# Rounds of four steps instead of two in a fused group-norm and displaced-convolution kernel

## What is computed

```python
# _gn(x): g = x in 32 groups; (g - mean(g)) / sqrt(var(g) + 1e-5)
disp = displace(_gn(x), round(offset))          # one offset for each of 48 groups of 8 channels
kernel = exp(-|field + offset - round(offset)|^2 / (2 * 0.5 ** 2)), normalised over 5 x 5
out = x + conv(disp, kernel)                    # depthwise, padding 2
```

## Time and profile before

| | us |
|---|---|
| median of 3 runs | 1166.61 |
| lowest and highest run | 1166.39, 1168.48 |
| the profiled execution | 1167.79 |
| its span in the trace | 1166.0 |

### The profile page before, as it was taken

One profiled execution on the slowest core, in us unless ns is written; L12 is line 12 of the kernel. 1 busy time (PEld: TensorE's weight loads), 2 busy tenths in 40 slices (PEclk: granted clock), 3 DMA queues, 4 the chain that ended last, 5 costly groups with the idle time before them and its releaser, 6 DMA issues.

```text
span 1166.0 us, 114171 instructions
## 1 busy us (share of the span) xinstructions
PE 1151.8 (99%) x50576; PEld 1125.5 (97%) x50576; DVE 953.2 (82%) x1373; ACT 785.5 (67%) x873; POOL 970.4 (83%) x1743
## 2 busy tenths in 40 slices
PE   9999999999999999999999999999999999999997
PEld 9899999999999999999999999999999999999997
DVE  8788888888888888888888888888888888888863
ACT  4676766667666676676767666676676766667664
POOL 7788888888888888888888888888888888888884
PEclk9999999999999999999999999999999999999999
DMA  8699999999999999999999999999999999999966
GB/s 273 237 383 382 364 355 369 359 358 358 349 360 356 355 361 352 359 355 357 355 354 358 353 357 358 352 359 356 353 356 353 358 350 363 359 347 362 353 212 211
DMA packets 409760, 402.93 MB, mean 346 GB/s; under 512 B 16528, under 2 KB 409744, under 8 KB 409744
## 3 DMA queue, kind: packets, MB, share of 16 engines
q1 hardware_dynamic: 204944, 201.41, 52.1%
q10 hardware_dynamic: 204800, 201.36, 50.0%
HBM read 201.38 MB, written 201.33 MB: 345 GB/s over the span
## 4 chain that ended last, share of the span: by engine, by line
PE 98%; issue 1%; POOL 0%; DVE 0%; DVEq 0%; POOLq 0%
PE ps L700 62%; PE ps L711 33%; PE ps L692 2%; PE ps L761 1%; DVE xin L513 0%; POOL var L308 0%; POOL rstd L310 0%; POOL ay L264 0%; POOL norm L326 0%; POOL ax L273 0%; DVE both L495 0%; POOL summands L286 0%; POOL spread L306 0%; POOL bias L312 0%; POOL inner L303 0%
## 5 line engine op out<-in xcount | busy, mean ns | idle before, releaser
L700 PE MATMUL ps<-ay,norm 32*128 32x128 f32 x24608 | 757.4, 275 | 1.0 <-DVEq L573 1.0
L700 PEld LDWEIGHTS ps<-ay,norm 32*128 32x128 f32 x24608 | 719.0, 187 | 9.7 <-ACTq L679 1.1
L485 DVE BATCH_NORM_STATS2 stats<-xin 128x6 f32<-128x512 f32 x768 | 488.7, 693 | 1.5 <-DMA xin<-in_x_dram 1.3
L624 ACT ACTIVATE y<-ps 128x1536 f32<-128x1536 f32 (+1 forms) x256 | 329.2, 1286 | 149.9 <-PE ps L700 149.7
L711 PE MATMUL ps<-ax,y 64*64 64x64 f32 x24576 | 392.1, 219 | 5.5 <-issue 5.4
L711 PEld LDWEIGHTS ps<-ax,y 64*64 64x64 f32 x24576 | 373.0, 135 | 22.6 <-issue 7.3
L326 POOL TENSOR_SCALAR norm<-xin,rstd,bias 128x768 f32<-128x768 f32 x256 | 296.5, 1159 | 104.3 <-PE ps L700 85.8
L513 DVE TENSOR_TENSOR xin<-ps,xin 128x1024 f32<-128x1024 f32 x256 | 313.2, 1224 | 82.9 <-PE ps L711 82.0
L613 ACT ACTIVATE norm<-xin,bias,rstd 128x768 f32<-128x768 f32 x256 | 263.0, 1027 | 168.6 <-DVE xin L513 82.5
L317 POOL TENSOR_TENSOR xin<-x,xin 128x512 f32<-128x512 f32 x256 | 321.0, 1276 | 7.6 <-ACT x L641 7.5
L641 ACT ACTIVATE x<-ps 128x512 f32<-128x512 f32 x256 | 150.5, 588 | 45.1 <-PE ps L711 45.0
(11 more groups left out here) (62 smaller groups left out, 273.4 us busy)
## 6 DMA issues: line engine op xcount, KB each, us to landing
xin<-in_x_dram SPq DMA_DIRECT2D x512, 384.0 KB, 6.9
out_dram<-xin ACTq DMA_DIRECT2D x512, 384.0 KB, 6.7
off<-in_L_conv_offset_dram SPq DMA_DIRECT2D x1, 48.0 KB, 3.2
```

Of the source, the lines that this page charges most:

```text
L485: nc.vector.bn_stats(stats[:, s // PAIR % RING, s % PAIR, n, :], xin[:, s].rearrange("p (g q) f -> p q f g", g=GROUPS)[:, n]).then_inc(bn_ ...
L624: nc.scalar.activation(y[:, v].rearrange("p k r a m -> p a (k r) m")[:, 0:lanes], ps[:, v, 0:lanes, 0:POS * P].rearrange("p a (n m) -> p a ...
L700: last = nc.tensor.matmul(ps[:, v, a, P * k:P * (k + 1)], norm[rows, v, r, P * k:P * (k + 1)], ay[rows, k, r, :], start=(r == 0), stop=(r ...
```

## The change

Rounds of four steps replace pairs of two. PE's outer loop (L825 after) does four first stages, in an inner loop of two passes, and then four second stages. `y` and `x2` get four homes instead of two; `ps` and `norm` keep two. Statistics, summands, sums and coefficients go by four steps: the small tiles are twice as wide. The product that sums the statistics has 72 columns instead of 36, and since it stands in the inner loop, it is done twice a round, of which DVE reads the second; its last matmul now also tells that the even first stage is done. The stores of a round stand in the next round, one before the first copy of y and one behind each of the other three. The normalisations of the next round's first two steps stand among the copies of the thirds. The column matrices (`ax`) are made in the new superblock's first round instead of at the end of the old. The tile for PE's idle products is made by ACT, and these products are fewer and narrower. Twelve loads instead of ten go out before the wait for the first products, and the extra first product behind the last step is gone.

```diff
-LEAD = 2
-AHEAD = PAIR * (LEAD + 2)
-RING = 4
-FIRST = 10
-BEHIND = 2
+QUAD = 4
+ROUNDS = STEPS // QUAD
+AHEAD = QUAD + 1
+FIRST = 12
...
+        y = sb("y", [P, QUAD, POS, R, LANES, 32])
+        x2 = sb("x2", [P, QUAD, QP, ROW])
+
+        stats = sb("stats", [P, 2, QUAD, CHUNKS, 3 * GROUPS])
+        summands = sb("summands", [P, QUAD, CHUNKS, 3 * GROUPS])
...
+        SPARE = 2
         IOTAS = 3 * LANES
...
+                    pool.wait_ge(bn_done, QUAD * CHUNKS * (quad + 1))
+
+                    if first:
+                        pool.wait_ge(stat_summed, 2)
+                    else:
+                        pool.wait_ge(y_done, QUAD * (quad - 1) + 1)
+                    number = quad + 2
...
-            def step(c, s, head, tail):
-                t, p = STEPS * c + s, STEPS // PAIR * c + s // PAIR
-                if not (tail and s + PAIR >= STEPS):
-                    normalise(t + PAIR, (s + PAIR) % STEPS, STEPS // PAIR * c + (s + PAIR) // PAIR)
-                if s % PAIR == 1:
-
-                    if not (tail and s // PAIR + LEAD + 1 >= STEPS // PAIR):
-                        make_summands(p + LEAD + 1, (s // PAIR + LEAD + 1) % RING)
-                    else:
-
-                        pool.engine_nop().then_inc(summands_ready, PAIR)
-                if s == STEPS - 1 and not tail:
-                    fill_rows(c + 1)
-                if s % PAIR == 1:
-                    if not (tail and s // PAIR + LEAD >= STEPS // PAIR):
-                        coefficients(p + LEAD, (s // PAIR + LEAD) % 2)
-                    add_third(t - 1, s - 1)
-                    add_third(t, s)
-                if s == STEPS - 1 and not tail:
-                    column_matrices(c + 1)
-            run(step)
+            coefficients(0, 0, early=1)
+
+            def one_round(c, g, first, last):
+                t, s, quad = STEPS * c + QUAD * g, QUAD * g, ROUNDS * c + g
+                if not first:
+                    add_third(t - 2, (s - 2) % STEPS)
+                normalise(t + 2, s + 2, quad, first)
+                if not first:
+                    add_third(t - 1, (s - 1) % STEPS)
+                if g == 0 and not first:
+                    column_matrices(c)
+                normalise(t + 3, s + 3, quad, first)
+                if last:
+
+                    pool.engine_nop().then_inc(summands_ready, QUAD)
+                else:
+                    make_summands(quad + 1, (g + 1) % 2, first=first)
+                    if first:
+                        pool.sem_inc(summands_ready, 2)
+                    coefficients(quad + 1, (g + 1) % 2, used=not first)
+                    normalise(t + 4, (s + 4) % STEPS, quad + 1)
+                    if g == ROUNDS - 1:
+                        fill_rows(c + 1)
+                    normalise(t + 5, (s + 5) % STEPS, quad + 1)
+                add_third(t, s)
+                add_third(t + 1, s + 1)
+                if last:
+                    add_third(t + 2, s + 2)
+                    add_third(t + 3, s + 3)
+            run(one_round)
...
+            def one_round(c, g, first, last):
+                t, s, quad = STEPS * c + QUAD * g, QUAD * g, ROUNDS * c + g
+                group_follows = c is not NSUPER - 1
+                for f in range(s + AHEAD, s + AHEAD + QUAD):
+                    if f >= STEPS and not group_follows:
+                        continue
+                    if f % QUAD == 0:
+
+                        if first:
+                            dve.wait_ge(first_summands, 2)
+                        else:
+                            dve.wait_ge(summands_ready, QUAD * quad + 2)
+                    all_statistics(c + f // STEPS, f % STEPS)
+                if group_follows:
+                    if g == 0:
+                        whole_distances(c + 1)
+                    if g == 1:
+                        full_distances(c + 1)
+                    if g == 3:
+                        values(c + 1)
+                if last:
+                    nc.vector.engine_nop().then_inc(sums_ready, QUAD)
+                else:
+                    sums(quad + 1, (g + 1) % 2, t + 2, read=not first)
+                copy_last_lane(t + 3)
+                if g == ROUNDS - 1 and group_follows:
+                    fill_image(c + 1)
+                for j in range(QUAD):
+                    add_x(t + j, s + j)
...
+                store_of_last_round(0)
+                copy_y(t, 0, first)
+                normalise(t + 2, s + 2, quad, first)
+                copy_y(t + 1, 1, first)
+                store_of_last_round(1)
+                normalise(t + 3, s + 3, quad, first)
+                copy_y(t + 2, 2, first)
+                store_of_last_round(2)
+                copy_y(t + 3, 3, first)
+                store_of_last_round(3)
+                border = g == ROUNDS - 1 and group_follows
                 if border:
                     fill_rows(c + 1, 0)
-                if s % PAIR == 1:
-                    copy_third(t - 1, s - 1, head and s == 1)
+                copy_third(t, s, first)
+                if not last:
+                    normalise(t + 4, (s + 4) % STEPS, quad + 1)
+                copy_third(t + 1, s + 1, first)
                 if border:
                     fill_rows(c + 1, 1)
-                    copy_third(t, s)
-                    normalise(t + PAIR, (s + PAIR) % STEPS, STEPS // PAIR * c + (s + PAIR) // PAIR, False)
-                if s >= BEHIND:
-                    store(c, s - BEHIND, t - BEHIND)
-                elif not head:
-                    store(c - 1, s - BEHIND + STEPS, t - BEHIND)
-                if not border and not (tail and s + PAIR >= STEPS):
-                    normalise(t + PAIR, (s + PAIR) % STEPS, STEPS // PAIR * c + (s + PAIR) // PAIR, False)
-                if s % PAIR == 1 and not border:
-                    copy_third(t, s, head and s == 1)
-                if not tail:
-                    if s == 5:
-                        square(c + 1, 0)
-                    if s == 7:
-                        square(c + 1, 1)
-                    if s == 9:
-                        exponential(c + 1)
-            run(step)
-
-            act.wait_ge(norm0_ready, TOTAL)
-            act.sem_inc(norm0_ready, 1)
-            act.wait_ge(mats_ready[0], TOTAL)
-            act.sem_inc(mats_ready[0], 1)
-            for s in range(STEPS - BEHIND, STEPS):
-                store(NSUPER - 1, s, TOTAL - STEPS + s)
+                copy_third(t + 2, s + 2, first)
+                if last:
+                    store(c, s, t)
+                else:
+                    normalise(t + 5, (s + 5) % STEPS, quad + 1)
+                copy_third(t + 3, s + 3, first)
+                if last:
+                    for j in range(1, QUAD):
+                        store(c, s + j, t + j)
+            run(one_round)
...
+                    last = nc.tensor.matmul(ps[:, v, a, place], ones[rows, :],
+                                            summands[rows, part].rearrange("p t n s -> p (t n s)"),
+                                            start=True, stop=True)
+                if early is None:
+
+                    last.then_inc(y_done, 1)
+                else:
+                    last.then_inc(stat_summed, 1)
...
+            def first_stages(one, number):
+
+
+                after = pe.snap(number + 1)
                 pe.wait_ge(x2_ready, one)
                 pe.wait_ge(result1_ready, one)
-                pe.wait_ge(norm0_ready, two)
-                y_product(0, 1)
-                pe.wait_ge(norm1_ready, two)
-                y_product(1, 1)
-                y_product(2, 1)
+                pe.wait_ge(y_ready, number)
+                y_even(number)
+                pe.wait_ge(summands_ready, number)
+                sum_stats(0)
+                second = pe.snap(one + 1)
+                pe.wait_ge(x2_ready, second)
+                pe.wait_ge(result1_ready, second)
+                pe.wait_ge(y_ready, after)
+                y_odd(after)
+
+            def second_stages(one):
                 pe.wait_ge(ax_ready, one)
                 pe.wait_ge(sums_ready, one)
-                pe.wait_ge(y_ready, one)
+                pe.wait_ge(y_ready, pe.snap(one + 4))
                 pe.sem_inc(x_started, 1)
                 x_products(0)
                 pe.wait_ge(last_lane_ready, one)
...
+                two = pe.snap(one + 2)
                 pe.wait_ge(x2_ready, two)
                 pe.wait_ge(result1_ready, two)
-                begin_even(three)
+                pe.sem_inc(x_started, 1)
+                x_products(2)
+                three = pe.snap(one + 3)
+                pe.wait_ge(x2_ready, three)
+                pe.wait_ge(result1_ready, three)
+                pe.sem_inc(x_started, 1)
+                x_products(3)
...
-                            nc.tensor.matmul(ps[:, v, a, POS * P + 36:512], idle[rows, :], idle[rows, 0:92],
```

(18 more changed lines are left out.)

309 lines of the change are left out of this document (144 added, 165 removed).

## The result

The changed kernel takes **1219.8 us** (median of 4 runs, 1218.6 to 1221.1) beside 1167.5 for the kernel before on the same chip: ratio 1.0448, 95% interval 1.0435 to 1.0461. That is 52 us slower, where I had forecast 6 us faster. The page of the profiled execution (span 1218.6): busy times, instruction packets, chain by engine, and the groups of the first stage's matmuls and weight loads.

A forecast was written before the change was run, and what follows sets the result against it. PE, busy 99% of the span, was taken as the bound. The terms -25.0 + 3.8 + 13.6 + 6.9 - 3.6 - 1.3 gave -5.6, so 1162.2, less 1.2: 1161 us, range 1154 to 1168.

The forecast's parts named there:

- (a): PE's stream: half of the shape changes between stages go, saving 0.39 us a round; -25.0 us (-18 to -32).
- (b): PE's sum product gets 72 columns, as often as before: 0.03 us a product, +3.8 us (0 to +7.7).
- (c): Within first stages, PE waits 0.22 us before y of t+3 for ACT's norm: +13.6 us (0 to +20).
- (d): Coefficients late for the second stages: PE waits 0.11 us before the round's last one, power taken as 1.84 us; +6.9 us.
- (e): Superblock borders: the late pair goes (-6.6), ACT's matrix fills delay copies of thirds (+3.0); -3.6 us.
- (f): Start: two instruction fetches in PE's first second-stage pass, and a wait behind a held load gone; -1.3 us (-5 to +4).
- (g): Hidden work: slot reuse after stores, DMA traffic at 357 GB/s, and DVE and POOL work stay covered, at no cost.
- the first: Rival: coefficients come in time (power near 1.02 us or a shorter chain), (d) is gone, 1154 us; chance 0.27.
- the second: Rival: the coefficients' chain is later, 6.3 us per 0.1 us; 1171 us if the reduction takes twice 0.31; chance 0.22.
- The third: Rival: the change of shape was not PE's overhead; (a) saves 18 instead of 25, 1168 us; chance 0.08.
- Instructions that don't stay in the store: Rival: PE's loop of 292 matmuls is fetched again once each round at 1.56 us, +98, 1259 us; chance 0.03.
- my signs of being wrong: A wait before every second stage, instruction packets after 60 us, or a period per round over 17.8 us.

The follow-up runs named there:

- e8: Changed kernel without its inner loop: one loop whose branch stands within a first stage, and norm waited for last; 1189.9 us (ratio 1.0184).
- e2: Changed kernel with the outer loop beginning with the second stages, so its branch stands behind a first stage; 1200.2 us (ratio 1.0276).
- e3: Changed kernel with six already fulfilled waits added at the end of each round, behind the second stages; 1238.8 us (ratio 1.0610).
- e4: Changed kernel with the same six fulfilled waits ahead of the last product of each odd first stage, twice a round; 1219.9 us (ratio 1.0444).
- b1: Kernel before, with the first product of y moved to the loop body's start, so the branch stands between second and first stages; 1203.0 us (ratio 1.0301).
- e11: e10 without the first of the round's two sum products; 1176.9 us (ratio 1.0061), runs scattered from 1167 to 1183.
- e1: Changed kernel with norm0 waited for last instead of first of three waits ahead of an even first stage; 1211.8 us (ratio 1.0387).
- e6: Changed kernel with ACT copying the third of step t+1 ahead of the normalisation of t+4; 1211.1 us (ratio 1.0375).
- e7: Changed kernel with POOL's power replaced by a subtraction, so the coefficients hold other numbers; 1215.1 us (ratio 1.0409).
- e12: e11 with the late loads of e9; 1172.1 us (ratio 1.0028, interval 1.0000 to 1.0056), scattered from 1163 to 1175.
- e9: Changed kernel with the loads of steps 12 to 15 held until three second stages are through; 1215.4 us (ratio 1.0414).
- e10: e8 with ACT's order of e6 (third of t+1 copied ahead of the normalisation of t+4); 1188.6 us (ratio 1.0185).
- e17: e10 with the round's fourth store issued behind the copy of the third of t+1 instead of behind the last copy of y; 1234.6 us (ratio 1.0569).
- e16: Kernel before with its stores issued by SyncE, each followed by the load of the slot stored six steps earlier; 1281.5 us (ratio 1.0981).

## Why the prediction was wrong

- **The step that failed** is one that the working didn't contain. In (a) I counted the changes of shape and what goes with them, and took each remaining one at its old price: the first stages would follow the second 0.15 us apart. That price held only as long as the loop's branch stood inside a first stage. The change moved it, an inner loop's set-up and the waits to the point where the queue has least lead. Cost: 0.51 us a round there, **+32 us** over 63 rounds (e8 takes it back to 0.15; e2, e3, e4 and b1 show the mechanism). In my list of the order of PE's queue the branches could be seen; I gave them no term.
- **(a)** What the missing changes gave back was 0.30 us a round, -19 instead of -25: 0.13 for second to first, 0.17 for first to second. It was the low end of the bounds. The range of the forecast, 1154 to 1168, was the spread of (a) alone; with the bounds of (b) and (c) as well it would have been 1137 to 1178, still far from 1219.8.
- **(b)** 36 more columns cost nothing: a sum product takes 0.18 us now and delays the records behind it by 0.05; before it was 0.14 and 0.08, the same 0.22. But that it is done twice a round for one use was there to be saved: e11 gained 12 us by it.
- **(c)** There is a wait, of 0.29 us a round instead of 0.22 (+19, not +13.6), but one step earlier: it stands at the inner loop's branch, before `y` of t + 2, and part of it is again PE's queue, which has its waits still to do once the normalisation is there (e1 takes 0.09 of it). Before `y` of t + 3, where I put it, the records run on. With the queue cured (e8) a wait of 0.14 does stand there, so the chain of (c) was real and hidden behind the larger wait.
- **(d)** was right in mechanism: the power went from 1.02 to 1.65 us, the reduction from 0.31 to 0.46 as taken, and PE comes 0.10 late a round at the fourth second stage, where I had 0.11; e6 gave 8.7 us and e7 4.7, against 6.9. The Trainium skill's rule (page "GPSIMD Engine Reference", section 3.1) would have made four more values 9 ns (the estimate from that page); measured were 0.63 us, 70 times that. The rows:

```profile
L324 POOL TENSOR_TENSOR rstd<-var,mhalf x65: 1015/1647/1724, 16.2 to 1185.1; 128x8 f32<-128x8 f32 x63, 128x4 f32<-128x4 f32 x2
...
L514 DVE TENSOR_REDUCE both<-ps 128x24 f32<-128x288 f32 x63 | 28.8, 458 | 155.1 <-ACT y L634 155.1
```

- **(e)** held in the two parts that it had: the late pair is gone (15 times 0.42, -6.3 against -6.6), and the rounds with ACT's fills take 0.21 more than the others (+3.1 against +3.0). But the rounds behind them, in which `ax` is now made, take 0.15 more (+2.3), for which I had nothing: -1 instead of -3.6.
- **(f)** was wrong by 10 us: +8.9 instead of -1.3. I counted two fetches at 1.56. There are four stops, 8.9 us in sum instead of 3.1, one of them among loads, and the lower clock behind that one costs 1.3 more.
- The end, which I set at nothing, costs 2.3. Behind the last copy of a third six DMA issues are left on ACT's queue (6.22 us from 1208.61) instead of four (3.49 us from 1158.79).
- **(g)** held in the changed kernel, not beyond it: at the 17.4 us rounds of e12 the traffic is 363 GB/s (500 to 560 us), 5% under the 383 of the earlier trace rows. Whether that costs PE time there isn't shown.

None of the rivals gives the time. The coefficients didn't come in time (the first), nor later than taken (the second); the second named the right direction, slower, by luck, since its chain isn't the cause. The third had (a) right, at 18 against 19, but that moves the sum by 6 us only. Instructions that don't stay in the store are refuted: 7 instruction packets instead of 4, six of them in the first 50 us, the last at 73.7, none after. Of my signs of being wrong, the round of over 17.8 us came true; the one packet after 60 us changes nothing.

**Left open.** What makes up the last 0.13 of the 0.51 us that neither b1 (0.31 for the branch alone) nor e2 (0.38) accounts for: the inner loop's set-up and its waits stand there too, but weren't moved alone; whether e12's scatter comes from the nearly full DMA engines or from ACT's queue; what e12 would give with its last round inside the loop (its peeled copy has three stops like e8's). None of this was tried.

## What to carry to other kernels

An instruction queue is a resource of its own: count branches, register operations and waits, fulfilled ones too, between the last product of one stage and the first of the next, and put loop ends where long products follow and precede (here: within a first stage). Fewer changes of stage are worth their own price only; before lengthening a round, look at which engine's queue would then have to do its work in one piece. Code executed for the first time stopped PE here, so peeled rounds weren't free (4.6 us for one stage of 384 records).

## What the runs showed of the hardware

- PE's queue: 0.11 us from one fulfilled wait instruction to the next, 0.21 for a branch that is taken; hidden within a first stage, exposed at either change of stages (the loop's branch: 0.38 us behind the 64 x 64 products, 0.24 ahead of them, e2). Six fulfilled waits, three instructions, cost 19 us in 64 rounds behind the 64 x 64 products and nothing within the first stage (e3, e4).
- The first execution of PE's code stopped it, mostly for 1.3 to 1.9 us, every 127 or 128 records, beside instruction packets of 16,384 bytes; once for 3.9 us while loads at 363 GB/s were in flight, 1.4 without them (e9).
- A DMA issue takes 0.62 us on ACT's queue, beside a running activation; the second issue of the fourth store 0.96 in e10, 0.77 in e12, and 0.62 in e17, where it comes later.
- POOL's power takes 1.02 us at four values a partition and 1.65 at eight; its neighbours 0.20 at either size.
- Loads and stores issued from a single queue, where they wait for one another, cost the kernel before 115 us (e16), for the same 403 MB.
